# Rotary q and k of an attention block projected as channels by tokens instead of tokens by channels and then turned

## The reference, cut to what matters

```python
def attention(x, kv_d_w, q_d_w, k_u_w, v_u_w, q_u_w, rope_k_w, rope_q_w, o_w):
    kv_d = x @ kv_d_w                                  # 512 -> 128
    q_d = x @ q_d_w                                    # 512 -> 128
    k_p = (kv_d @ k_u_w).reshape(b, s, NH, RD)         # 128 -> 256, RD = 16 plain channels a head
    q_p = (q_d @ q_u_w).reshape(b, s, NH, RD)
    v = (kv_d @ v_u_w).reshape(b, s, NH, HD)           # 128 -> 512
    k_r = (x @ rope_k_w).reshape(b, s, NH, RD)         # 512 -> 256, RD = 16 rotary channels a head
    q_r = (q_d @ rope_q_w).reshape(b, s, NH, RD)
    k = concatenate([k_p, apply_rope(k_r, cos, sin)])  # x * c + concatenate([-x2, x1]) * s, x1 and x2 halves of 8
    q = concatenate([q_p, apply_rope(q_r, cos, sin)])
    probs = softmax(causal(q @ k.T / sqrt(HD)))
    return (probs @ v) @ o_w
```

## Time and profile before

| | us |
|---|---|
| median of 3 runs (lowest, highest) | 1253.35 (1252.35, 1255.59) |
| the profiled execution | 1256.78 |
| its span, first to last instruction | 1255.0 |
| mean granted TensorE clock, share of 2.4 GHz | 0.960 |
| busy: PE, DVE, ACT, POOL | 1145.3, 728.1, 572.9, 333.9 |

### The profile page before, as it was taken

How to read it: one execution, slowest core, us unless ns; L and a number is a source line. 1 busy time by engine, 2 the same in 40 slices (tenths; PEclk the granted TensorE clock), 3 DMA queues, 4 the chain that set the end, 5 groups by cost and what they waited for, 6 DMA issues and landing times.

```text
span 1255.0 us, 18112 instructions
## 1 busy us (share of the span) xinstructions
PE 1145.3 (91%) x5687; PEld 798.4 (64%) x5687; DVE 728.1 (58%) x1714; ACT 572.9 (46%) x1248; POOL 333.9 (27%) x275
## 2 busy tenths in 40 slices
PE   5989989999999899999989899989989999999960
PEld 5755545665666456557657667755657888888850
DVE  6465486468545865656646766574545764444433
ACT  3324365445544565555455555544456743222310
POOL 0413133201320231002022202200235644555530
PEclk9969999999999899999989999998999999999985
DMA  7153344336322742553584473486567735656569
GB/s 262 34 168 118 98 145 130 90 98 202 120 64 89 228 131 64 184 168 105 175 229 140 144 247 95 144 250 162 145 215 249 250 126 106 109 111 116 106 147 328
DMA packets 105609, 191.10 MB, mean 152 GB/s; under 512 B 24140, under 2 KB 34796, under 8 KB 103980
## 3 DMA queue, kind: packets, MB, share of 16 engines
q1 hardware_dynamic: 96700, 169.61, 43.7%
q0 software_dynamic: 8512, 19.93, 8.9%
q10 hardware_dynamic: 304, 0.40, 0.1%
HBM read 118.98 MB, written 65.53 MB: 147 GB/s over the span
## 4 chain that ended last, share of the span: by engine, by line
PE 73%; DMA 8%; DVE 7%; SPq 4%; issue 3%; ACT 3%; POOL 1%; DVEq 0%; ACTq 0%; POOLq 0%
PE psum L976 12%; PE psum L793 9%; PE psum L794 8%; PE psum L795 8%; PE psum L939 6%; PE psum L960 6%; PE psum L1054 4%; PE psum L1056 4%; PE psum L1055 4%; PE psum L802 3%; PE psum L1081 2%; SPq L554 2%; PE psum L1083 2%; PE psum L1082 2%; PE psum L1023 2%
## 5 line engine op out<-in xcount | busy, mean ns | idle before, releaser
L1298 ACT ACTIVATE probs<-psum 128x512 f32<-128x512 f32 (+3 forms) x512 | 257.4, 517 | 217.2 <-PE psum L963 108.9
L1722 DVE TENSOR_REDUCE nmax<-psum 128x1 f32<-128x512 f32 x256 | 171.3, 686 | 124.2 <-PE psum L939 119.4
L939 PE MATMUL psum<-stack 96*128 96x512 f32 (+3 forms) x512 | 211.0, 417 | 10.1 <-DVE nmax L1725 6.7
L976 PE MATMUL psum<-probs,vals 128*33 128x512 f32 (+3 forms) x1024 | 212.3, 537 | 0.0
L960 PE MATMUL psum<-stack 97*128 97x512 f32 (+3 forms) x512 | 199.7, 391 | 11.8 <-ACT probs L1298 6.2
L1725 DVE CUSTOM_DVE_ANT_0 psum<-psum,causal 128x128 f32<-128x128 f32 (+3 forms) x256 | 123.8, 503 | 74.6 <-PE psum L939 73.6
L939 PEld LDWEIGHTS psum<-stack 96*128 96x128 f32 x512 | 100.5, 196 | 83.2 <-issue 58.4
L960 PEld LDWEIGHTS psum<-stack 97*128 97x128 f32 x512 | 99.7, 195 | 38.8 <-ACT probs L1298 16.7
L1433 POOL TENSOR_TENSOR o_lo<-o_chunk,o_hi 128x512 fp32r<-128x512 f32 x31 | 42.0, 1354 | 276.4 <-ACT o_hi L1140 276.4
L976 PEld LDWEIGHTS psum<-probs,vals 128*33 128x33 f32 x1024 | 50.0, 112 | 101.5 <-issue 76.4
L793 PE MATMUL psum<-w_hi,xh 128*128 128x512 f32 (+1 forms) x256 | 96.8, 378 | 5.2 <-POOL xl L1401 3.6
(11 more groups left out here) (245 smaller groups left out, 2283.1 us busy)
## 6 DMA issues: line engine op xcount, KB each, us to landing
stack<-split_s SPq DMA_DIRECT2D x378, 128.0 KB, 3.3
split_s<-split SPq DMA_DIRECT2D x64, 512.0 KB, 3.9
inverse_sums<-inverse_s SPq DMA_DIRECT2D x31, 256.0 KB
xt<-in_x_dram SPq DMA_DIRECT2D x4, 1024.0 KB, 5.3
x_s<-yt SPq DMA_DIRECT2D x4, 1024.0 KB, 5.6
xt<-x_s SPq DMA_DIRECT2D x4, 1024.0 KB, 5.3
res<-x_s SPq DMA_DIRECT2D x4, 1024.0 KB, 10.3
yt<-in_x_dram SPq DMA_DIRECT2D x4, 1024.0 KB, 6.0
```

What stands on the lines that cost most here:

```text
L939: sq.filled(nc.tensor.matmul(psum[:, sq.bank(M), 0:n], st[:, 0, t * P:(t + 1) * P], st[:, 1, 0:n], start=True, stop=True), M)
L976: nc.tensor.matmul(psum[at_:at_ + VW, o.bank(p), lo:S], vals[k % 2][:, t, head_of(q, side), :], probs[:, M % NX, lo:S], start=(t == 0), st ...
L1298: sk.cleared(nc.scalar.activation(probs[:, M % NX, lo:S], psum[:, sk.bank(M), lo:S], ACT.Exp, scale=SCALE), M)
L1722: sq.cleared(V.tensor_reduce(out, psum[:, sq.bank(M), :], AX.X, ALU.max, negate=True), M)
```

## The change

q and k of phase 2 are now computed as channels by tokens. There are eight products, `part`: for k and for q, the plain channels of heads 0 to 7 and of heads 8 to 15 (a = 0, 1) and the first and the second rotary halves of all 16 heads (a = 2, 3), each 128 channels by 512 tokens. The host lays the columns of the rotary weights out by halves. The plain parts get a high and a low part as the turns did. A rotary part is multiplied by cos and by sin straight from its PSUM bank, on DVE, which then frees the bank. POOL subtracts or adds the terms (`rot`), ACT rounds the high parts two steps later, POOL subtracts for the low parts (`rot_lo`). The eight turns are gone. SP stores eight parts of 512 KB in place of the eight turns, plain ones two steps after their product, rotary ones two steps after `rot_lo`. The store in DRAM is doubled, by parity of the batch. The tables of cos and sin are 128x512 each and are loaded at k = 3, m = 2. The `v` products and some steps of norm2, x2, router, square and scale move by a few steps.

```diff
+PARTS = (("k", 0), ("k", 1), ("k", 2), ("k", 3), ("q", 0), ("q", 1), ("q", 2), ("q", 3))
+ROT_LO = 3
+PART_STEPS, ROT_STEPS, V_STEPS = (6, 8, 9, 12, 15, 17, 20, 21), (21, 27), (26, 35, 38, 42)
...
-            put(((43, 43, 44, 44) if k == NB - 1 else (36, 37, 38, 39)), each("norm2", i, 4))
+            put(((43, 43, 44, 44) if k == NB - 1 else (35, 36, 37, 38)), each("norm2", i, 4))
...
-            put(((51, 52, 54, 55) if k == NB - 1 else (45, 47, 48, 50)), each("x2", i, NC))
-            put(((59, 62) if k == NB - 1 else (55, 57)), each("router", i, 2))
+            put(((51, 52, 54, 55) if k == NB - 1 else (46, 48, 49, 51)), each("x2", i, NC))
+            put(((59, 62) if k == NB - 1 else (56, 58)), each("router", i, 2))
...
         put((1, 4), [("kv_d", j), ("q_d", j)])
-        for n in range(2 * NT):
-            put((6 + 2 * n, 7 + 2 * n), [("qk", j, n), ("rope", j, n)])
-        put((23, 27, 35, 39), each("v", j, NT))
-        for g, m in enumerate(((30, 32), (37, 40), (45, 48), (55, 56))):
-            put(m, turns(j, g))
+        put(PART_STEPS, each("part", j, len(PARTS)))
+        put(ROT_STEPS, [("rot", j, c) for c in "kq"])
+        put([m + ROT_LO for m in ROT_STEPS], [("rot_lo", j, c) for c in "kq"])
+        put(V_STEPS, each("v", j, NT))
...
-            put((14, 16, 20, 22), square)
+            put((13, 15, 19, 21), square)
...
-            put((31, 35, 36, 39), scale)
+            put((31, 35, 36, 37), scale)
...
-    split_s = dram("split_s", (NG, P, 4, S))
+    split_s = dram("split_s", (2, NG, P, 4, S))
...
+            def store_part(j, n):
+
+                c, a = PARTS[n]
+                if n == 0:
+                    for p in range(NPR):
+                        wait_stack(sp, NPR * (j - 2) + p)
+                if a < 2:
+                    ring.wait_read(sp, ("part", j, n))
                 else:
+                    sp.wait_ge(rot_lo, 4 * (j - B) + rotary_no(c, a - 2) + 1)
...
+                sp.dma_start(to[heads, rows, role:role + 2, :],
+                             (split[:, 2 * a:2 * a + 2, :] if a < 2 else rotated[rotary_no(c, a - 2)][:, :, :]).bitcast(F32))\
+                    .then_inc(part_st[a] if a < 2 else rot_st, 16)
...
-                    sp.wait_ge(stored, 16 * split_no(k, q // 2))
+                    if k < B:
+                        sp.wait_ge(stored, 16 * split_no(k, q // 2))
+                    else:
+                        sp.wait_ge(part_st[n], 16 * 2 * (k - B + 1))
+                        sp.wait_ge(rot_st, 16 * 4 * (k - B + 1))
...
+                elif kind == "part":
...
+                    if a < 2:
+                        product(key, [w2((W2_KU if c == "k" else W2_Q) + a * P, P)], [latent("kq".index(c), slice(0, S))])
+                    elif c == "k":
+                        product(key, [rotary(W2_D + n * 512 + 256, a - 2) for n in range(NC)], chans())
                     else:
+                        product(key, [rotary(W2_Q + 256, a - 2)], [latent(1, slice(0, S))])
...
+                elif kind == "rot":
+                    c, = at_
+                    for a in range(2):
+                        act.wait_ge(rot_add, 4 * (j - B) + rotary_no(c, a) + 1)
+                        n = rotary_no(c, a)
+                        copy(rotated[n][:, 0, :], terms[n][:, 1, :]).then_inc(rot_hi, 1)
...
+                elif kind == "rot":
+                    c, = at_
+                    n = 4 * (j - B) + rotary_no(c, 0)
+                    pool.wait_ge(rot, 2 * n + 4)
+                    for a, op in enumerate((ALU.subtract, ALU.add)):
+                        t_ = terms[rotary_no(c, a)]
+                        nc.gpsimd.tensor_tensor(t_[:, 1, :], t_[:, 0, :], t_[:, 1, :], op).then_inc(rot_add, 1)
+                elif kind == "rot_lo":
...
+                        pool.wait_ge(rot_hi, 4 * (j - B) + n + 1)
+                        nc.gpsimd.tensor_tensor(rotated[n][:, 1, :], terms[n][:, 1, :], rotated[n][:, 0, :].bitcast(F32),
+                                                ALU.subtract).then_inc(rot_lo, 1)
...
+                elif kind == "part":
+                    c, a = PARTS[at_[0]]
+                    if a < 2:
+                        lo_of(key, split[:, 2 * a, :], split[:, 2 * a + 1, :])
                     else:
+                        ring.wait_full(dve, key)
...
+                        bank = psum[:, ring.bank(key), :]
+                        for x in range(2):
+                            V.tensor_tensor(terms[rotary_no(c, (a - 2) ^ x)][:, x, :], bank, rope[:, x, :], ALU.mult).then_inc(rot, 1)
+                        dve.wait_ge(rot, 2 * n + 2)
+                        dve.sem_inc(ring.free[RING_NO[key] % 2], 1)
```

More of the change, by code:

```diff
@@ L160, with rotary_no, is_plain @@
 LAST = NB - 1
+def rotary_no(c, half):
+    return 2 * "kq".index(c) + half
+def is_plain(key):
+    return key[0] == "part" and PARTS[key[2]][1] < 2
 def is_value(key):
@@ L170, in later @@
     if engine == "ACT":
-        return LAG_VALUE if is_value(key) else 0
+        return LAG_ROT if key[0] == "rot" else LAG_VALUE if is_value(key) else 0
     if key[0] == "w2":
         return LAG_W2
-    return LAG_LO if key[0] in ("x", "turn", "kv_d", "q_d", "x2") and not is_value(key) else 0
+    return LAG_LO if is_plain(key) or key[0] in ("x", "turn", "kv_d", "q_d", "x2") and not is_value(key) else 0
 def steps_of(engine):
@@ L240, in numbered @@
     return {key: n for n, key in enumerate(x for x in IN_ORDER if kinds(x))}
-RING_NO = numbered(lambda x: x[0] in ("max", "x", "qk", "v", "turn", "kv_d", "q_d", "back", "turn_o", "out", "x2", "router", "upto"))
+RING_NO = numbered(lambda x: x[0] in ("max", "x", "qk", "part", "v", "turn", "kv_d", "q_d", "back", "turn_o", "out", "x2", "router", "upto"))
 VALUE_NO = numbered(is_value)
-HI_NO = numbered(lambda x: x[0] in ("kv_d", "q_d", "turn_o", "x2") or x[0] in ("x", "turn") and x not in VALUE_NO)
+HI_NO = numbered(lambda x: is_plain(x) or x[0] in ("kv_d", "q_d", "turn_o", "x2") or x[0] in ("x", "turn") and x not in VALUE_NO)
 DIVIDED = [(k, c) for k in range(NB) for c in range(NC) if not by_turns(k, 2 * c)]
@@ L356, in build @@
         assert heads_.where == TILES_AT + TILES_SIZE
+        turned = Strip(TILES_AT)
+        rope = turned("rope", [P, 2, S])
+        terms_at = [turned.where + n * 8 * S for n in range(3)]
+        assert terms_at[-1] + 8 * S <= TILES_AT + 4 * NT * 2 * D
         tiles = Strip(TILES_AT)
@@ L386, in build @@
         vals = [rest(f"vals{n}", [P, NT, H, VW]) for n in range(2)]
+        terms_at.append(rest.where)
         vs = rest("vs", [P, 2, S])
+        terms = [at(f"rope_terms{n}", terms_at[n], [P, 2, S]) for n in range(4)]
+        rotated = [at(f"rotated{n}", terms_at[n], [P, 2, S], F32R) for n in range(4)]
         stack = rest("stack", [P, 2, NSTK, S], F32R)
@@ L453, in build @@
         v_ok, v_hi, v_lo = sem("value_ready"), sem("value_hi"), sem("value_lo")
-        qk_ok = sem("qk_copied")
         hsq, hsum = sem("head_squares"), sem("head_square_sums")
         h_sc = sem("heads_scaled")
-        rot_in, rot, rot_add = sem("rotary_inputs"), sem("rotary_terms"), sem("rotary_added")
+        rope_ld, rot, rot_add = sem("rope_tables_loaded"), sem("rotary_terms"), sem("rotary_added")
+        rot_hi, rot_lo = sem("rotated_hi"), sem("rotated_lo")
+        part_st, rot_st = [sem(f"parts_stored{i}") for i in range(2)], sem("rotated_stored")
         k_st, q_st = sem("split_k_stored"), sem("split_q_stored")
@@ L687, in _ @@
                             {"k": store_k, "q": store_q}[key[3]](*key[1:3])
+                        if is_plain(key):
+                            store_part(*key[1:])
+                    for key in BESIDE[k].get(m - 2, ()):
+                        if key[0] == "rot_lo":
+                            for n, part in enumerate(PARTS):
+                                if part[0] == key[2] and part[1] >= 2:
+                                    store_part(key[1], n)
+                    if k == B - 1 and m == 2:
+                        ring.wait_full(sp, ("turn", B - 1, NG - 1, "q"))
+                        for n, src in enumerate((cos_d, sin_d)):
+                            sp.dma_start(rope[:, n, :], src).then_inc(rope_ld, 16)
                     for next_, q in loads_at(m):
@@ L830, in w2d, with latent, rotary @@
                 return [w2(W2_D + c * 512 + at_, n) for c in range(NC)]
-            def latent(n, t):
-                return kqh[:, n, t * P:(t + 1) * P], kql[:, n, t * P:(t + 1) * P]
+            def latent(n, at_):
+                return kqh[:, n, at_], kql[:, n, at_]
+            def rotary(at_, half):
+                return w2(at_ + half * P, P)
             def beside(key):
@@ L2019 @@
     data["rope_cos"], data["rope_sin"] = rope_tables()
+    for name in ("L0_ffn_rope_k_w", "L0_ffn_rope_q_w"):
+        halves = np.asarray(inputs[name]).reshape(-1, H, 2, RD // 2)
+        data[name] = halves.transpose(0, 2, 1, 3).reshape(-1, H * RD)
```

111 lines of the change are left out of this document (42 added, 69 removed).

## The result

The changed kernel takes 1259.7 us, median of 20 runs (1255.34 to 1266.58), against 1255.75 us for the kernel before, median of 20 (1250.5 to 1259.83). The ratio is 1.0039, with a 95% interval of 1.0025 to 1.0053: slower by some 5 us, where 15 us less were forecast. The profiled execution took 1260.65 us with a span of 1258.9.

What follows compares the result with a forecast made beforehand. PE was taken to bound most of a batch, DVE one stretch of k = 5 and 6. 12.8 + 3.4 + 1.0 - 1.0 - 0.8 = 15.4 us less than 1253.35 gave 1238, range 1227 to 1251.

Steps and rivals of the forecast that it cites:

- Part 4 (c): SP's eight 512 KB stores a batch at new steps, and two table loads in k = 3: counted as zero.
- rival E: PE with less to do falls to 1.2 GHz in k = 3, 4 and 6: 16 us lost, no change, chance 0.09.
- T3: Theory of the experiments, not the prediction: the half clock that follows stalls makes them dearer.
- Rival D: SP blocked at steps 26 and 32 by rotary stores waiting for POOL: 19 us lost, 1257, slower, chance 0.09.
- Part 4: What is added: 1.0 us for held banks, 0.8 for POOL's longer work, zero for stores and pair loads.
- Part 1: The turns go from PE, 8 a batch in 4 batches at 0.40 us each: 12.8 us less.
- Part 2: PE's q and k products, 10.2 us a batch before and 10.1 after, still in steps 6 to 21: nothing.
- Part 3: Other engines: 3.4 us from DVE's stretch and bank waits in k = 5 and 6, 1.0 from k = 4's stall.
- Part 4 (a) and (b): Rotary parts' banks held longer by DVE, 1.0 us lost; POOL's longer work holding up DVE's divides, 0.8 lost.
- rival C: Held banks and POOL's collisions cost 10 us, the DVE stretch gives nothing: 6 less, 1247, chance 0.10.
- rival B: DVE stretch and k = 4 stall give everything, no cost appears, small gaps close: 24 less, 1229, chance 0.14.

Runs made afterwards that it cites:

- e1: The changed kernel with plain parts of all 16 heads, so their stores are 16-wide, not 8: 1240.17 us, ratio 0.9895.
- e5: The changed kernel with 16-wide plain stores for k alone, q's staying 8-wide: 1243.12 us, ratio 0.991.
- e9: The changed kernel with 16-wide stores, later rotary stores, and yt loaded at step 13 in k = 5 and 6: 1231.88 us, ratio 0.9829.
- e7: The changed kernel with 16-wide stores, later rotary stores, later divide of the last heads, and yt loaded at step 13: 1238.96 us, ratio 0.9869.
- e2: The changed kernel with SP issuing the rotary stores later, at steps 29 and 33: 1254.05 us, ratio 0.9998.
- e12: e9 with norm2, x2 and router of phase 2 back at the steps of the kernel before: 1229.36 us, ratio 0.9812.

## Why the prediction was wrong

**The step that failed is Part 4 (c)**, "the same eight stores of 512 KB a batch ... Zero". They were the same in bytes and number, not in shape. Before, a store's destination had 128 rows outermost and the store 16 completions; the plain part's has 8 heads and 9 completions. The diff shows this in one line (`heads, rows = (slice(8 * a, 8 * a + 8), ...`), and the prediction read only the size. And the moved stores were priced without a look at what SP issues behind them: at step 8 the inverse sums' store, at step 10 the row of step 12 and the inverse sums. The term counted at zero measured 18 us by e1, and e5 puts 16 of them on k's two stores.

The Trainium skill has the rule (DMA: Bandwidth & Descriptors, Why a DMA increments its semaphore by 16 and not by 1, and again in Rules for kernel authors): the number of engines that a DMA uses is set by the slowest dimension that isn't 1 of its two access patterns, and an outermost size below 16 confines the whole DMA to at most that many engines. The traces agree: 9 completions for a store with 8 outermost (by the page one for each of 8 engines, and the rest of the 16 written at once: the first of the 9 comes 1.1 us after the issue, the others from 4.7 us on), 16 for one with 16, and 6.0 to 8.1 us against 4.1 to 5.8. Held against the diff, this rule would have forbidden the zero.

How 8 us of stalls became 16: in the rows of steps 6 to 21 PE is idle (length less busy time) 0.8 us before, 8.8 after and 0.3 in e1. And the same matmuls are busy 103.1 us after and 95.1 in e1, 8.0 more. The clock accounts for that: it was 0.94, 0.88 and 0.87 in k = 4 to 6, 1.00 before. At a mean of 0.88 a share of 0.24 ran at 1.2 GHz, 7 us of the 29.3, and half of them, 3.5, is the loss; the three batches give an estimated 1.7, 3.5 and 3.6, together 8.8 us. So the clock took about half. This is **rival E's** mechanism with another trigger: not less work on PE, but gaps in it. Its point against itself, that k = 6 kept 1.00 through 3.3 us of gaps, is true as well, and k = 3 after the change kept 1.00 with 0.7 us of them in these steps; no run shows what sets the gaps apart that the clock falls behind. That less work alone lowers the clock is not seen where it can be read without stalls: over steps 22 to 40, without the turns, e9 is at 1.00 in all four batches, as the kernel before. In steps 41 to 58 the clock is lower in e9 (0.93 and 0.87) than before (0.94 and 1.00), but 1.00 in both in e7; that stays open. T3 was not tested apart from the stalls.

**Rival D** came true in k = 5 and 6 at 5 us in all at most (e2), a quarter of its price, and not in k = 3 and 4. It had SP, the queue behind it and the right symptom. It gave itself too much to spare: step 40 of k = 6 begins at 813.99, not 814.9, and the row of 809.33 took 3.5 us to land, not 2, so 1.2 us were to spare and not 3.5. It looked for the lateness in ACT's copies and POOL's sum; it was the yt load, which lands in 12 us where it took 5.3 to 5.9, with a store of q now right ahead of it. Part 4 named what is behind SP, but not what is ahead of `rot_lo` on POOL.

**Part 1, right.** No transposes from `qk` are left in k = 3 to 6 (128 before). Step 40 of k = 6 takes 0.50 us where it took 0.85, and in e9 steps 30, 32 and 37 of k = 3 to 6 are 0.38 to 0.44 shorter. Over steps 22 to 40, with four turns a batch, the kernel before has 33.1, 29.3, 30.7 and 30.5 us for k = 3 to 6 and e9 has 30.8, 27.3, 28.8 and 27.6: 9.1 less, where the turns' 6.4 and two bank waits of 0.4 were counted. 2.9 of the 9.1 didn't go but moved: one of the four v products (3 x 0.24 us a batch) now stands at step 42. That leaves 6.2, close to the turns' 6.4. (The row named steps 30 to 39 is steps 31 to 40; it changes nothing in this.)

**Part 2, right.** Steps 6 to 21 in e1: 95.4 us against 95.9.

**Part 3, about right in its larger term, at full clock, and too high in the smaller.** The DVE stretch, steps 41 to 58 at a clock of 1.00: 26.1 us before, 22.9 to 23.3 with the change's steps, about 3 less a batch. The four turns there make 1.6, and the v product moved in costs 0.7, so DVE's relief was worth about 2 us a batch, where 1.7 were counted (which was to hold step 35 too). e12 gives 1 us more, but by the old steps, which aren't the change's. In e9 itself the two stretches are only 3.1 us shorter together, since the clock is at 0.93 and 0.87: there the clock took back about half. DVE's busy time there fell by 3.6 and 3.9. The stall in k = 4 was to give 1.0: the load of the inverse sums before step 51 takes 5.2 us, not 5.4, and their store 2.5, not 3.2; step 51 keeps 2.79 of its 3.19 us. So it was for the most part not the turns' stores that made it late. Its last sentence, "What is late next is the same chain of three DMAs ... whose steps stay", named exactly the chain that broke, at step 16 instead of 51, and gave it no price.

**Part 4 (a) and (b), right in kind and priced too high.** The multiplications take 686 ns, counted at 685:

```profile
L1695 DVE TENSOR_TENSOR rope_terms<-psum,rope 128x512 f32<-128x512 f32 x32 | 20.6, 686 | 25.9 <-PE psum L844 25.9
L1490 POOL TENSOR_TENSOR rotated<-rope_terms,rotated 128x512 fp32r<-128x512 f32 x16 | 20.2, 1284 | 25.1 <-ACT rotated L1191 25.1
```

Steps 6 to 21 of e1 leave PE idle for 0.3 us in all four batches, so the banks that they held cost nothing. The divide's mean fell from 977 to 785 ns, so POOL's longer work met it less often, not more; by rival C both were to cost 10 us, and no cost shows. That fits what the prediction took from the Trainium skill (SBUF — State Buffer, Who interferes with whom) as far as the multiplications go: 686 ns each, beside a POOL that works longer.

**The sum.** With the stores' shape right and D's cause mended, the change is worth 21 us (e9, 0.9829): above the 15.4 forecast and near rival B's 24. The 6 us beyond the forecast are not traced to single terms; they are no proof that the forecast's terms were too small, since the clock alone moves a stretch by as much. With the shape alone right the change is worth 13 (e1). The terms for the work removed were sound; the change as it was made lost more than all of it, through one term at zero and a smaller one, POOL's wait for yt, that no part named.

## What to carry to other kernels

Price a moved or rewritten DMA by its shape as well as its bytes: look at the outermost size of both sides, and at what is issued on the same queue while it is on its way (6 to 8 us here). Small transfers that something waits for (a row, a broadcast of sums) must not stand behind a narrow store; here two such stores a batch cost 16 us and the mending was a permutation of columns. When a wait for one engine is put into a queue, ask what that engine itself waits for ahead of it, a load in the case here.
